# The first gate product of the next slot between the last two down products: one edit of order in a two-block transformer kernel

## The chip, the cores and the metric

The kernel runs on one core of one Trainium2 chip. The metric is the device time of one execution in microseconds (us), as the median of repeated runs. Lower is better.

## The reference, cut to what matters

Sixteen batches of 512 tokens with 128 features pass through two blocks. The change touches only the first:

```
x = x + 0.5 * moe(norm(x))       # shared expert and 16 routed experts, top 2, silu gates
x = x + lin_attn(norm(x))        # linear attention with rotated keys and queries
x = x + 0.5 * moe(norm(x))       # the same weights again
x = x + 0.5 * relu_mlp(norm(x))  # 128 -> 512 -> 128
x = x + softmax_attn(norm(x)); x = x + 0.5 * relu_mlp(norm(x))   # second half of the kernel
```

In the mixture (moe), for one pair of experts or the shared one: `y += (silu(x @ Wg) * (x @ Wu) * routing) @ Wd`. The routing weights come from a sigmoid of the router's logits, the best two of 16, and their share of the sum.

## The kernel before, in words

The front part (`build_front`) does the first four lines above for all batches, the back part the rest. The front is a chain of **slots**. One slot is one mixture layer of one batch (the main work), with the linear attention or the ReLU layer of another batch woven in (the side work). Four slots make a turn: `SIDE = [ATT, MLP, ATT, MLP]`; eight turns make 32 slots, with one slot without side work ahead (number -1) and one behind. Below, "attention slot" and "MLP slot" are named by their side work.

A slot has `NT` = 9 steps, n = 0 to 8: step 0 is the shared expert, steps 1 to 8 a pair of routed experts each. A step has these parts, and each engine's order is written out by hand:

- TensorE (PE): the gate product into bank `G[n % 2]`, the up product into bank `U` (three matmuls of 512 columns each, because the operands are split into a high and a low part), the routing weights of the pair into `C`, and, one step late, the down product of step n-1 (`moe_down`, four transposed matmuls that the trace shows as eight) into `Y`.
- ScalarE (ACT): `s = silu(G)`, line 514.
- VectorE (DVE): `su = U * s` (`activated`, line 668, which writes `h[0]` in step 0), then `h = C * su` (`routed`, line 677).

Around them stand, for the side work of the same slot: row statistics of `xw` on DVE (`side_parts`, line 565, and `total`, line 572), the power on GpSimd (POOL, lines 384 to 390), `zs` on ACT (line 473), `side_transposes` on PE (line 875), `xhs` on ACT, `xls` on DVE (line 690), and then the products that read `xhs` and `xls` (`kvu_product`, line 899, in an attention slot; `hidden`, line 832, into `S[1]` in an MLP slot, followed by `mlp_down` into `S[0]` two steps later). For the main work of the next slot: statistics (`main_stats`), `z` on POOL (lines 377 to 399), `main_transposes` on PE (line 817) in step 3 of an attention slot and step 4 of an MLP slot, `xh`, `xl`, the router logits, their `exp` on ACT (`scores`, line 469), and the top-two choice on DVE (`routing_scores` to `routing_weights`, lines 605 to 654), which ends in `comb_transposes` on PE (line 857) in step 0 of the next slot. `main_residual` (line 681) closes the slot on DVE; `side_parts` of the next slot follows it there.

Every engine takes its instructions strictly in the written order, and semaphores carry the waits between engines: `gate_ready`, `act_done`, `up_ready`, `up_used`, `h_ready`, `down_done` count steps.

Of the kernel before, what the change touches and what calls it, by code (L numbers as in the profile page):

```python
# [33 lines left out]
NT = TE + 1  # L34
FT = 4
# [116 lines left out]
def build_front(nc, weights, early, x_dram, mid_dram, ident_dram, staged_dram, tail_dram, turns):  # L152
    w = weights
    with ExitStack() as ctx:
# [301 lines left out]
        @block.scalar  # L456
        def _(act):
            def main_high(q, i):

                act.wait_ge(zT_ready.sem, zT_ready.at(i, q + 1))  # L460
                nc.scalar.activation(xh[q % 2][:], Z[:], ACT.Copy).then_inc(xh_ready.sem, 1)

            def logits_half(q, i):
                act.wait_ge(logits_ready.sem, logits_ready.at(i, q + 1))
                nc.scalar.activation(lb[:], Z[:, :, E:2 * E], ACT.Copy).then_inc(lb_ready.sem, 1)

            def scores(q, i):
                act.wait_ge(lg_ready.sem, lg_ready.at(i, q + 1))
                nc.scalar.activation(en[:], lg[:], ACT.Exp, scale=-1.0).then_inc(score_ready.sem, 1)

            def normalise(out, src, scale, off):
                for t in range(T):
                    ins = nc.scalar.activation(out[:, t], src[:, t], ACT.Identity, bias=off[:, t:t + 1],
                                               scale=scale[:, t:t + 1])
                return ins

            def side_normalise(m, i, k):
                act.wait_ge(srstd_ready.sem, srstd_ready.at(i, k + 1))
                normalise(zs, xw[SIDE_BATCH[m]], rstd_s, off_s).then_inc(sz_ready.sem, 1)

            def out_normalise(a, i):
                act.wait_ge(rstd2_ready.sem, rstd2_ready.at(i, a + 1))
                normalise(on, S[1], rstd2, off2).then_inc(on_ready.sem, 1)

            def side_high(i, k):
                act.wait_ge(szT_ready.sem, szT_ready.at(i, k + 1))
                nc.scalar.activation(xhs[:], S[0][:], ACT.Copy).then_inc(xhs_ready.sem, 1)

            def hidden(m, k, i):
                act.wait_ge(hid_mm.sem, hid_mm.at(i, FT * nth(m) + k + 1))  # L490
                nc.scalar.activation(hs[k % 2][:], S[1][:], ACT.Relu,  # L491
                                     bias=w["b1"][:, k:k + 1]).then_inc(hid_ready.sem, 1)

            def first_batch(n):
                if n == 4:
                    act.wait_ge(first_xt.sem, 1)
                    nc.scalar.activation(xhs[:], Z[:], ACT.Copy).then_inc(first_xh.sem, 1)
                if n == 6:
                    act.wait_ge(first_kp.sem, 1)
                    nc.scalar.activation(early.khi[:], S[0][:], ACT.Copy).then_inc(early.khi_ready.sem, 1)  # L500
                    act.wait_ge(first_qp.sem, 1)
                    nc.scalar.activation(early.qhi[:], S[1][:], ACT.Copy).then_inc(early.qhi_ready.sem, 1)
                if n == 8:
                    act.wait_ge(first_v.sem, 1)
                    nc.scalar.activation(early.va[:, :, :, 0:DH], Z[:].rearrange("p t (h e) -> p t h e", h=H),
                                         ACT.Copy)

            def slot(m, i, side, prepare):
                g0, steps = NT * m, PREPARE[side or MLP]
                for n in range(NT):  # L510
                    act.wait_ge(gate_ready.sem, gate_ready.at(i, g0 + n + 1))
                    if n >= 2:
                        act.wait_ge(up_used.sem, up_used.at(i, g0 + n - 1))
                    nc.scalar.activation(sbuf_s[n % 2][:], G[n % 2][:], ACT.Silu).then_inc(act_done.sem, 1)  # L514
                    if n == 0:
                        act.wait_ge(combT_ready.sem, combT_ready.at(i, m + 1))
                        nc.scalar.activation(cT[m % 2][:], Z[:], ACT.Copy).then_inc(cT_ready.sem, 1)
                    if n == 0 and side == MLP:
                        act.wait_ge(oT_mm.sem, oT_mm.at(i, nth(m - 1) + 1))
                        nc.scalar.activation(oT[:], S[0][:], ACT.Copy).then_inc(oT_ready.sem, 1)  # L520
                    if n == 1 and side:
                        side_normalise(m, i, m)
                    if n == 2 and side:
                        side_high(i, m)
                    if side == ATT:
                        a = nth(m)
                        if n == 4:
                            act.wait_ge(kvu_out.sem, kvu_out.at(i, T * (a + 1)))
                            nc.scalar.activation(kvu[:, :, 0:D], kvu[:, :, 0:D], ACT.Silu).then_inc(ka_ready.sem, 1)
                            act.wait_ge(q_mm.sem, q_mm.at(i, a + 1))  # L530
                            nc.scalar.activation(qa[:], S[1][:], ACT.Silu, bias=w["bq"][:]).then_inc(qa_ready.sem, 1)
                        if n == 7:
                            out_normalise(a, i)
                    elif side == MLP:
                        if 3 <= n < 3 + FT:
                            hidden(m, n - 3, i)
                    if prepare:
                        if n == steps["transpose"]:
                            main_high(m + 1, i)
                        if n == steps["logits"]:  # L540
                            logits_half(m + 1, i)
                        if n == steps["logits"] + 1:
                            scores(m + 1, i)
                    else:
                        first_batch(n)

            main_high(-1, 0)
            logits_half(-1, 0)
            scores(-1, 0)
            slot(-1, 0, None, True)  # L550
            for i in range(turns):
                for m in range(NM):
                    slot(m, i, SIDE[m], True)
            slot(0, turns, None, False)

        @block.vector
        def _(dve):
# [188 lines left out]

            def slot(m, i, side, before, prepare):
                a, steps = nth(m), PREPARE[side or MLP]
                if side:
                    side_parts(m, i)  # L750
                if not prepare:
                    first_stats()
                for n in range(NT):
# [2 lines left out]
                    activated(m, n, i)  # L756
                    if n == 0:
                        if side:
                            total(stats_s, mv_s, smv_ready)
                        if before == MLP:  # L760
                            side_residual(NM - 1 if m == 0 else m - 1, i - 1 if m == 0 else i)
                    else:
                        routed(m, n, i)
# [46 lines left out]
        def _(pe):  # L810
# [121 lines left out]
            def first_batch(n):  # L932
# [9 lines left out]
                if n == 7:  # L942
# [4 lines left out]
                                       skip_group_check=True)  # L947
                    mm.then_inc(first_v.sem, 1)

            def slot(m, i, side, prepare):  # L950
                g0, a, steps = NT * m, nth(m), PREPARE[side or MLP]
                high, low = xh[m % 2], xl[m % 2]
                pe.wait_ge(xl_ready.sem, xl_ready.at(i, m + 1))
                for n in range(NT):
                    if n >= 2:
                        pe.wait_ge(act_done.sem, act_done.at(i, g0 + n - 1))
                    product(G[n % 2], w["wgh"][:, n], w["wgl"][:, n], high, low).then_inc(gate_ready.sem, 1)
                    if n >= 1:
                        pe.wait_ge(up_used.sem, up_used.at(i, g0 + n))
                    product(U, w["wuh"][:, n], w["wul"][:, n], high, low).then_inc(up_ready.sem, 1)  # L960
                    if n == 0:
# [5 lines left out]
                    if n == 1 and side == MLP:  # L967
                        pe.wait_ge(oT_ready.sem, oT_ready.at(i, nth(m - 1) + 1))
                        down(S[1], oT, w["wout"][:], True).then_inc(side_mm.sem, 1)
                    if n == 2 and side:  # L970
                        side_transposes(i, m)
                    if n == 3 and side:
                        side_input(i, m)
# [5 lines left out]
                        if n == 6:  # L979
                            attend(a, i)  # L980
                    if side == MLP:
                        if 5 <= n < 5 + FT:
                            mlp_down(m, n - 5, i)
                        if 3 <= n < 3 + FT:
                            hidden(m, n - 3, i)
# [6 lines left out]
                    if n >= 1:  # L992
                        moe_down(m, n - 1, i)
                    if side == ATT:
                        if n == 4:
                            queries(a, i)
                        if n == 5:
                            keys_values(a, i)
                moe_down(m, NT - 1, i)

            main_transposes(-1, 0)
            logits(-1, 0)
            slot(-1, 0, None, True)
            for i in range(turns):
                for m in range(NM):
# [884 lines left out]
```

## Time and profile before

| | |
|---|---|
| median of 3 runs | 1994.09 us (1993.52 to 1995.16) |
| the profiled execution's own time | 1994.67 us |
| its span in the trace | 1992.6 us, 34534 instructions |
| granted TensorE clock, mean | 0.989 |
| PE busy over the span | 1886.7 us (95%) |
| DVE busy | 1540.8 us (77%) |
| ACT busy | 1176.8 us (59%) |
| POOL busy | 670.6 us (34%) |
| one MLP and one attention slot together, start to start | 66.3 us, the mean of the 15 periods between line 681's first and last start (106.2 to 1100.5 us) |
| window 566 to 632 us, one MLP and one attention slot | PE 64.11, DVE 46.71, ACT 28.83, POOL 23.45 us busy of 66.00; granted clock 1.00 |

The span begins with the first instruction and ends with the last; what lies between span and time is start and end of the execution. The slots of the front lie between about 41 and 1161 us. PE has two rows: the matmuls, whose ends are modelled, and the weight loads (PEld) ahead of them. A wait shows in square brackets with the engine that ended it. Two matmuls that follow each other are best compared by their starts.

### The profile page before, as it was taken

How to read it: one execution, taken by the hardware profiler on the slowest of the kernel's cores; microseconds unless marked ns; L12 is line 12 of the kernel's file. 1: busy time of each engine (PE TensorE's matmuls, PEld its weight loads, DVE VectorE, ACT ScalarE, POOL GpSimd, SP SyncE). 2: the span in 40 equal slices, each digit the busy share in tenths (PEclk: the TensorE clock that was granted, in tenths of full speed). 3: DMA queues.
4: the chain of work that ended last, by engine and by line, in shares of the span. 5: the costliest groups of instructions: out<-in, count | busy, mean ns of one | idle time of the engine just before them, and what ended most of it. 6: DMA issues, size and time to landing. Idle time of an engine off the chain costs nothing. (4 is left out here: it accounts for less than half of the span.)

```text
span 1992.6 us, 34534 instructions
## 1 busy us (share of the span) xinstructions
PE 1886.7 (95%) x12468; PEld 1312.5 (66%) x12468; DVE 1540.8 (77%) x3888; ACT 1176.8 (59%) x2210; POOL 670.6 (34%) x766
## 2 busy tenths in 40 slices
PE   2999999999999999999999989999999999999997
PEld 1888888888888888888888844444444444444443
DVE  5766866686668666866676669999999999999991
ACT  2344444444444444444444428888888888888884
POOL 2333433343334333433343223333333333333311
PEclk9999999999999999999999969999999999999998
DMA  3000000000000000000010022222232222222210
GB/s 131 7 12 1 12 11 12 1 12 12 11 1 11 12 12 1 11 12 12 1 38 6 7 85 86 86 88 90 91 92 86 86 90 93 90 87 86 86 44 11
DMA packets 49992, 85.81 MB, mean 43 GB/s; under 512 B 6752, under 2 KB 11104, under 8 KB 49760
## 3 DMA queue, kind: packets, MB, share of 16 engines
q1 hardware_dynamic: 47920, 81.85, 13.2%
q8 instruction: 99, 1.62, 0.3%
q10 hardware_dynamic: 1904, 1.78, 0.3%
q14 instruction: 69, 0.57, 0.1%
HBM read 49.26 MB, written 34.87 MB: 42 GB/s over the span
## 5 line engine op out<-in xcount | busy, mean ns | idle before, releaser
L1490 DVE TENSOR_REDUCE b_nm<-b_MX 128x1 f32<-128x512 f32 x1024 | 652.0, 684 | 44.6 <-PE b_MX L1598 24.5
L1383 ACT ACTIVATE b_pr<-b_ST 128x512 f32<-128x512 f32 x1024 | 552.4, 611 | 92.0 <-PE b_ST L1586 89.9
L514 ACT ACTIVATE s<-G 128x512 f32<-128x512 f32 x306 | 182.5, 596 | 350.7 <-PE G L834 348.0
L839 PE MATMUL Y<-w_wd,h 128*128 128x128 f32 x2448 | 329.2, 277 | 17.4 <-DVE h L677 16.1
L668 DVE TENSOR_TENSOR su<-U,s 128x512 f32<-128x512 f32 x272 | 187.1, 688 | 191.4 <-PE U L834 112.8
L839 PEld LDWEIGHTS Y<-w_wd,h 128*128 128x128 f32 x2448 | 305.8, 192 | 33.2 <-DVE h L677 23.9
L1598 PE MATMUL b_MX<-b_kt,b_qt 32*128 32x512 f32 x768 | 236.5, 504 | 2.4 <-DVE b_nm L1490 2.4
L1586 PE MATMUL b_ST<-b_qt,b_kt 32*128 32x512 f32 x768 | 214.7, 494 | 2.8 <-ACT b_pr L1383 1.5
L1586 PEld LDWEIGHTS b_ST<-b_qt,b_kt 32*128 32x128 f32 x768 | 83.1, 181 | 195.0 <-ACT b_pr L1383 141.1
L677 DVE TENSOR_TENSOR h<-C,su 128x512 f32<-128x512 f32 x272 | 188.1, 692 | 9.3
L832 PE MATMUL G<-xh,w_wgh 128*128 128x512 f32 x306 | 145.2, 475 | 0.0
L384 POOL TENSOR_TENSOR vpe_s<-mv_s,w_eps 128x4 f32<-128x4 f32 x32 | 6.4, 199 | 404.1 <-DVE mv_s L572 404.1
L1613 PE MATMUL b_PV<-b_pr,e_va 128*32 128x512 f32 x1024 | 138.1, 612 | 0.0
L1613 PE MATMUL b_PV<-b_pr,b_va 128*32 128x512 f32 x1024 | 136.4, 605 | 0.0
L832 PE MATMUL U<-xh,w_wuh 128*128 128x512 f32 x306 | 123.9, 405 | 9.5 <-DVE su L668 9.5
L834 PE MATMUL G<-xl,w_wgh 128*128 128x512 f32 x306 | 121.1, 396 | 0.0
L833 PE MATMUL G<-xh,w_wgl 128*128 128x512 f32 x306 | 121.0, 395 | 0.0
L834 PE MATMUL U<-xl,w_wuh 128*128 128x512 f32 x306 | 120.7, 395 | 0.0
L833 PE MATMUL U<-xh,w_wul 128*128 128x512 f32 x306 | 120.0, 392 | 0.0
L867 PE MATMUL C<-cT,w_pairs 128*128 128x512 f32 x272 | 107.7, 396 | 0.0
L1598 PEld LDWEIGHTS b_MX<-b_kt,b_qt 32*128 32x128 f32 x768 | 95.5, 184 | 10.2 <-DVE b_nm L1490 5.0
L491 ACT ACTIVATE hs<-S,w_b 128x512 f32<-128x512 f32 x64 | 44.0, 687 | 94.6 <-PE S L834 94.6
(295 smaller groups left out, 3705.6 us busy)
## 6 DMA issues: line engine op xcount, KB each, us to landing
b_kt<-staging SPq DMA_DIRECT2D x48, 256.0 KB, 3.1
b_qt<-staging SPq DMA_DIRECT2D x48, 256.0 KB, 3.5
staging<-e_khi SPq DMA_DIRECT2D x32, 256.0 KB, 2.9
staging<-e_qhi SPq DMA_DIRECT2D x32, 256.0 KB, 2.9
xin<-in_x SPq DMA_DIRECT2D x17, 256.0 KB, 2.8
mid<-xo SPq DMA_DIRECT2D x16, 256.0 KB, 2.0
staging<-e_klo SPq DMA_DIRECT2D x16, 256.0 KB, 2.9
staging<-e_qlo SPq DMA_DIRECT2D x16, 256.0 KB, 2.9
```

The lines of the kernel that those rows point to most:

```text
L514: nc.scalar.activation(sbuf_s[n % 2][:], G[n % 2][:], ACT.Silu).then_inc(act_done.sem, 1)
L668: nc.vector.tensor_tensor(out[:], U[:], sbuf_s[n % 2][:], ALU.mult).then_inc(up_used.sem, 1)
L677: nc.vector.tensor_tensor(h[n % 3][:], C[:], su[n % 2][:], ALU.mult).then_inc(h_ready.sem, 1)
L832: pe.matmul(flat(bank), wh, flat(high), start=True, stop=False)
L833: pe.matmul(flat(bank), wl, flat(high), start=False, stop=False)
L834: return pe.matmul(flat(bank), wh, flat(low), start=False, stop=True)
L839: mm = pe.matmul(bank[:, t], hid[:, t], wd, start=(first and t == 0), stop=True, skip_group_check=True)
L1383: nc.scalar.activation(pr[k % 2][:, j], bank[:].rearrange("p a b -> p (a b)"), ACT.Exp, scale=SM_SCALE).then_inc(used["st"].sem, 1)
L1490: nc.vector.tensor_reduce(nm[g % 2][:, c:c + 1], bank[:].rearrange("p a b -> p (a b)"), AX.X, ALU.max).then_inc(used["mx"].sem, 1)
L1586: pe.matmul(flat(bank_of(B, "st", 0, u)), kt_[g][rows_of(j), k % T], flat(qt[g])[rows_of(j)], start=True, stop=True).then_inc(made["st"].s ...
L1598: pe.matmul(flat(bank_of(B, "mx", rel, u)), qt[g][rows_of(j), u // HG % T], flat(kt_[g])[rows_of(j)], start=True, stop=True).then_inc(made ...
L1613: mm = pe.matmul(flat(PV)[rows_of(j)], va[B.parity][:, kt, g * HG + j], pr[k % 2][:, j], start=(kt == 0), stop=(kt == T - 1), skip_group_c ...
```

## The change

Six edits of order, no arithmetic added or removed:

1. PE: the gate product of step 0 of the next slot is issued between the last two down products of this slot (`gate(m + 1, 0, i)` ahead of `moe_down(m, NT - 1, i)`). It waits for `xl` of the next slot and for the silu of step 8, which reads the same bank.
2. ACT: the silu of step 0 waits for `up_used` of the last step before it, because it writes `s[0]`.
3. PE: in an MLP slot the last `mlp_down` moves from behind `C` of step 8 to between the gate and the up product of step 8.
4. PE: in an attention slot `side_transposes` moves from ahead of `moe_down` of step 1 to behind it (both in step 2).
5. ACT: `scores` (the exponential) moves ahead of the side work of its step; in an MLP slot that is ahead of the last `hidden` activation.
6. DVE: `side_parts` moves from ahead of the first product of the slot (`activated`, n = 0) to behind it.

```diff
 (scalar)
+                    elif n == 0 and up_used.at(i, g0) > 0:
+                        act.wait_ge(up_used.sem, up_used.at(i, g0))
                     nc.scalar.activation(sbuf_s[n % 2][:], G[n % 2][:], ACT.Silu).then_inc(act_done.sem, 1)
...
                     if n == 2 and side:
                         side_high(i, m)
+                    if prepare and n == steps["logits"] + 1:
+                        scores(m + 1, i)
...
                         if n == steps["logits"]:
                             logits_half(m + 1, i)
-                        if n == steps["logits"] + 1:
-                            scores(m + 1, i)
 (vector)
-                if side:
-                    side_parts(m, i)
...
                     activated(m, n, i)
                     if n == 0:
                         if side:
+                            side_parts(m, i)
                             total(stats_s, mv_s, smv_ready)
 (tensor)
+            def gate(m, n, i):
+                g0 = NT * m
+                if n >= 2:
+                    pe.wait_ge(act_done.sem, act_done.at(i, g0 + n - 1))
+                elif n == 0:
+                    pe.wait_ge(xl_ready.sem, xl_ready.at(i, m + 1))
+                    if m >= 0:
+                        pe.wait_ge(act_done.sem, act_done.at(i, g0))
+                product(G[n % 2], w["wgh"][:, n], w["wgl"][:, n], xh[m % 2], xl[m % 2]).then_inc(gate_ready.sem, 1)
...
-                pe.wait_ge(xl_ready.sem, xl_ready.at(i, m + 1))
                 for n in range(NT):
-                    if n >= 2:
-                        pe.wait_ge(act_done.sem, act_done.at(i, g0 + n - 1))
-                    product(G[n % 2], w["wgh"][:, n], w["wgl"][:, n], high, low).then_inc(gate_ready.sem, 1)
                     if n >= 1:
+                        gate(m, n, i)
+                        if side == MLP and n == NT - 1:
+                            mlp_down(m, FT - 1, i)
                         pe.wait_ge(up_used.sem, up_used.at(i, g0 + n))
...
-                    if n == 2 and side:
+                    if n == 2 and side == MLP:
                         side_transposes(i, m)
...
-                        if 5 <= n < 5 + FT:
+                        if 5 <= n < 4 + FT:
                             mlp_down(m, n - 5, i)
...
                     if side == ATT:
+                        if n == 2:
+                            side_transposes(i, m)
...
+                if prepare:
+                    gate(m + 1, 0, i)
                 moe_down(m, NT - 1, i)
...
             logits(-1, 0)
+            gate(-1, 0, 0)
             slot(-1, 0, None, True)
```

## Rows read from the trace of the kernel before

**Rows 1.** Waits of PE's weight loads, 0 to 1140 us: total, times, longest.

```profile
PEld Y L839 <- DVE h L677: 23.3, 33, 1.2
PEld U L832 <- DVE su L668: 16.9, 17, 1.0
PEld Z L817 <- POOL z L399: 15.6, 18, 8.9
```

**Rows 2.** Timeline at an attention slot's end: start, duration, engine, line, operation.

```profile
568.15 1.27 POOL L438 TENSOR_TENSOR og<-og,ub 128x512 f32<-128x512 f32 x1
568.57 0.93 DVE L646 TENSOR_TENSOR first<-first,second 128x64 f32<-128x64 f32 x1
568.71 1.16 PE L839 MATMUL Y<-w_wd,h 128*128 128x128 f32 x8 [0.92 <-DVE h L677]
...
570.27 0.68 DVE L681 SCALAR_TENSOR_TENSOR xw<-Y,xw 128x512 f32<-128x512 f32 x1
...
570.99 0.87 DVE L565 BATCH_NORM_STATS2 stats_s<-xw 128x6 f32<-128x128 f32 x4
...
571.78 0.67 DVE L668 TENSOR_TENSOR h<-U,s 128x512 f32<-128x512 f32 x1
...
572.47 0.28 DVE L572 BATCH_NORM_AGGREGATE mv_s<-stats_s 128x2 f32<-128x6 f32 x3
```

**Rows 3.** Timeline of the MLP slot after it, step 4.

```profile
582.82 1.04 POOL L399 TENSOR_TENSOR z<-z,rstd 128x512 f32<-128x512 f32 x1
...
583.91 0.42 PEld L817 LDWEIGHTS Z<-w_ident,z 128*128 128x128 f32 x4 [0.32 <-POOL z L399]
```

**Rows 4.** Timeline of steps 5 to 8 of that MLP slot, and the next slot's start.

```profile
589.77 0.23 DVE L597 TENSOR_TENSOR lg<-Z,lb 128x64 f32<-128x64 f32 x1 [1.40 <-ACT lb L465]
...
593.72 0.69 ACT L491 ACTIVATE hs<-S,w_b 128x512 f32<-128x512 f32 x1 [1.92 <-PE S L834]
...
594.43 1.28 ACT L469 ACT_TABLE_LOAD   x1
...
596.01 0.20 DVE L605 TENSOR_SCALAR en<-en 128x64 f32<-128x64 f32 x1 [2.64 <-ACT en L469]
...
597.74 0.48 PE L832 MATMUL G<-xh,w_wgh 128*128 128x512 f32 x1
...
599.24 0.50 PE L832 MATMUL U<-xh,w_wuh 128*128 128x512 f32 x1 [0.56 <-DVE su L668]
...
602.34 0.97 PEld L839 LDWEIGHTS Y<-w_wd,h 128*128 128x128 f32 x8 [0.27 <-DVE h L677]
...
603.25 0.48 PE L832 MATMUL G<-xh,w_wgh 128*128 128x512 f32 x1
...
604.03 0.40 PE L832 MATMUL U<-xh,w_wuh 128*128 128x512 f32 x1
```

**Rows 5.** Timeline of the attention slot after that, steps 0 to 3.

```profile
606.81 1.05 PE L839 MATMUL Y<-w_wd,h 128*128 128x128 f32 x8
...
607.62 0.48 PE L832 MATMUL G<-xh,w_wgh 128*128 128x512 f32 x1
...
608.18 0.86 DVE L565 BATCH_NORM_STATS2 stats<-xin 128x6 f32<-128x128 f32 x4
...
609.18 0.28 DVE L572 BATCH_NORM_AGGREGATE mv<-stats 128x2 f32<-128x6 f32 x3
...
609.81 0.63 PE L875 MATMUL S<-w_ident,zs 128*128 128x128 f32 x4 [0.33 <-ACT zs L473]
...
611.51 0.68 DVE L690 TENSOR_TENSOR xls<-S,xhs 128x512 fp32r<-128x512 f32 x1
...
612.79 0.33 PE L899 MATMUL S<-w_wkvuh,xhs 128*128 128x384 f32 x1
```

**Rows 6.** ACT's groups in the back part, 1165 to 1992 us: count, busy time, mean ns.

```profile
L1372 ACT ACTIVATE b_hid<-b_MX,w_b 128x512 f32<-128x512 f32 x68 | 48.0, 705 | 5.0 <-PE b_MX L1521 4.8
...
L1383 ACT ACT_TABLE_LOAD x1 | 1.3, 1283 | 0.0
```

## The prediction, made before the change was run

> **What bounds the kernel now.** I read the page first: TensorE is busy 95% of the span, and the diff touches only the front, so the question is what TensorE's few idle moments in the front are. A view of busy shares cannot say it; the waits can, and the list of PE's weight loads says it better than that of the matmuls, since a matmul's modelled end hides a short wait. [rows 1] are that list for the front. The reader is to see three sorts of wait and their counts: the last down product of a slot waits for `h` (33 times, 23.3 us), an up product waits for `su` 17 times (16.9 us), and the transposes of `z` wait for POOL 18 times (15.6 us, of which 8.9 us is one wait at the very start). 17 and 33 say "once per MLP slot" and "once per slot"; 18 less the start and the slot ahead of the turns is again once per MLP slot. So the third wait is the small one, 0.32 us [rows 3], but it says most: it shows that in every MLP slot a chain of other engines arrives at PE just after PE does.
>
> I then read the timeline of one pair (the pairs are alike, so one stands for 16). At an attention slot's end PE starts the last down product at 568.71 after 0.92 us of idling [rows 2]. At an MLP slot's end there are two gaps: the up product of step 8 starts at 599.24, 1.50 us after the gate product's start at 597.74, where a product takes 0.78 from the first start to the next (603.25 to 604.03), so 0.72 is lost; and the last down product is loaded at 602.34 after a wait of 0.27 [rows 4]. In the attention slot, the side transposes wait 0.33 for `zs` at 609.81 [rows 5].
>
> **The chain beside PE.** Behind an attention slot's end, nothing on DVE starts from PE. `main_residual` starts at 570.27, not when `Y` is done (568.71 + 0.8 of starts + 0.4 for the last matmul = 569.9) but when the routing work of `comb` is through; and that was held by POOL: DVE's small product of line 646 took 0.93 us, from 568.57 to 569.50, and POOL's `og` ran to 569.42 [rows 2]. From there it goes on without a pause that PE ends: row statistics, POOL's power, `zs`, the silu of step 2 behind `zs`, `su`, `h`, `xls`, the statistics of the next main batch, POOL again, and `z` is through at 582.82 + 1.04 = 583.86; PE loads it at 583.91 [rows 3]. `og` itself goes back to `attend` in step 6 of the attention slot through statistics, POOL and ACT. So from `attend` to the transposes of `z`, over a third of each pair is a latency chain, and PE's 0.92 us there is slack that this chain makes, wherever PE takes it.
>
> **The change part by part.** Prices first: a gate product 0.78 behind a down product, a down product 0.81 (606.81 to 607.62) [rows 4, 5], `C` 0.23 (a third of a product).
>
> *Attention slot's end, 16 times.* The gate product (0.78) fills the idle 0.92. It waits for the silu of step 8, which has run before `su` and `h` of that step, for which PE waits anyway; so it fits, and the last down product stays at 568.71. The next slot's up product starts about 0.7 earlier. But the chain does not. `main_residual` stays at 570.27. Then `side_parts` no longer stands ahead of `activated`: before, from 570.27 to the end of the aggregates is 572.75 - 570.27 = 2.48 [rows 2]. After, `activated` starts at 570.99 (the up product, started at about 569.6, delivers 0.54 + 0.40 later plus a hop, 570.65, so it is in time), the statistics 0.61 later, and from the start of the four statistics to the end of the aggregates is 609.46 - 608.18 = 1.28 [rows 5]: 0.72 + 0.61 + 1.28 = 2.61. The chain gets 0.13 longer, and arrives at PE at 584.04. PE, 0.7 early, gives it back, 0.3 to 0.4 at the side transposes and the rest at `z`: the price is 0.13 us, **a loss of 0.13 per pair**, not a gain of 0.7. Without edit 6, `activated` would stay at 571.78 and hold the second up product; so edit 6 is what lets PE run ahead, and what lengthens the chain.
>
> *MLP slot, from `z` to the last down product.* The exponential moves into ACT's idle 1.92 ahead of the last `hidden` activation at 593.72: load 1.28 and 0.26 of work make 1.54 [rows 4], and its input is there since 590.00 (589.77 + 0.23). DVE's `routing_scores`, which sat idle 2.64 until 596.01 [rows 4], can run about 2.3 earlier, with POOL idle, so nothing holds it. So `su` of step 7 is no longer late, the up product of step 8 does not wait, and the last but one group of eight small DVE operations no longer stands ahead of `su` of step 8. The work from the gate product at 597.74 to the last down product is then gate 0.78, `mlp_down` 0.81, up 0.78, `C` 0.23, down 0.81, next gate 0.78 = 4.19, against 602.34 - 597.74 = 4.60 now, though it holds a gate product more. `h` of step 8 is ready at 4.03 + a hop: `su` starts at 1.59 + 0.94 + 0.09 = 2.62, and two DVE products of 0.7 follow. No wait, by 0.1. **Gain 0.41 per pair.** Edit 3 alone would cover the up product's gap too, so the two overlap; if the exponential gained nothing, `su` of step 8 would stay where DVE puts it and this term would be 0.
>
> One cost could hide here: whether ACT needs another table for the Relu behind the exponential. In the back part 68 Relus run among the exponentials with one table load in all [rows 6], so no. The Trainium skill (ScalarE: Activation LUTs, "What ACT_TABLE_LOAD costs") puts a switch at 1.28 us of load plus 1.38 us of drain, which would speak against switching in front of `hidden`. Here the load starts at 594.43, 0.02 after the activation before it ended (593.72 + 0.69) [rows 4], so the trace has the first part and not the second. By the page's price, an estimate, the silu of step 7 would come some 2.8 us later than I have it, still about when it runs now, and `su` of step 8 0.1 late: 16 x 0.1 = 1.6 us less of gain.
>
> *MLP slot's end to the attention slot's `kvu` products.* Here the chain starts from PE's last down product. Before, 602.34 to the end of `xls` is 611.51 + 0.68 - 602.34 = 9.85, and PE is there at 612.79, 10.45 [rows 4, 5], with 0.6 of slack. After, PE has one gate product less (0.78, done before) and no wait of 0.33 to 0.5 at the transposes, since edit 4 puts a down product of 0.81 there; it would be there at 9.2. The chain takes 9.85 + 0.13 + 0.05 = 10.03. So PE waits about 0.8 in all, at the transposes and at `xls`, and the **gain is 10.45 - 10.03 = 0.42 per pair**. `z` is asked for a stage later in this slot, with no wait in [rows 1], and stays behind the `kvu` products. From `kvu` to `attend` everything follows PE, and POOL's products, the slowest there, end ahead of PE: unchanged.
>
> *Edges.* The slot ahead of the turns gains the last term once (its exponential had no Relu to wait for). The last MLP slot is followed by a slot that keeps its statistics ahead of `activated`: its second up product waits for that, and the 0.42 turns into about -0.2. The other waits of edits 1 and 2 are met before: 0.
>
> Sum: 16 x (0.41 - 0.13) + 16 x 0.42 - 0.2 = 4.5 + 6.7 - 0.2 = 11.0. I bound the terms: the first between -0.9 (below) and +0.7, the second between 0 and 1.1 (0.72 + 0.27 + a refill of 0.1), the third between -0.3 and 0.8 + 0.42. The profiled time is 1994.67 us, so 1983.6; the median is 0.58 lower and I take the same step: 1994.1 - 11 = **1983.0 us**.
>
> **The rivals.**
>
> *Every filled gap is won* (a reader of the waits alone would say this): 0.7 at the attention end, 1.1 at the MLP end, 0.4 at the side transposes, 2.2 x 16 = 35, giving 1959. Against it stands the wait for `z` [rows 1, 3]: where it is there already, an earlier PE only waits longer. 6%.
>
> *The chain behind an attention slot is not as rigid*: if edit 6 or the port's release starts it earlier by what PE is early, the first term is +0.4 to +0.7 instead of -0.13: 11 + 16 x 0.7 = 22, giving 1972. For it speaks only that the chain has some twenty hops that I add up from one execution. 9%.
>
> *The statistics behind the first product push the whole chain* (the other side). My 0.13 stands on `activated` starting right behind `main_residual`. If it starts as late as now (because the up product or the silu of step 0 is late), the four statistics add their full 0.9: first term -0.9, third -0.3, second +0.41: -0.8 x 16, giving 2007. It decides at 0.5 us of lengthening, where the sum 0.41 - x + 0.55 - x is zero. The up product has 0.3 to spare at the attention end and none at the MLP end. 8%.
>
> *The gain is given back on the way*: the second term is 0 (DVE's order holds `su` of step 8) and half of the third goes to a wait in the attention slot: 16 x (0.2 - 0.13) = 1, giving 1993, no change that can be told. 8%.
>
> **How the numbers follow.** The likeliest, 69%, has its own range of 1979 to 1989 (each of the three terms off by 0.1 to 0.2). A measurement here tells a change from none at about 0.2%, 4 us. Faster: 69 + 6 + 9 = 84%, and a little of it may fall short: 83%. Same 8%, slower 9%. Leaving out the widest two (1959 and 2007) and half a case more, the range is 1971 to 1991.
>
> **What would show it.** After: the gate product of step 0 stands ahead of the last down product; PE's wait for `h` nearly gone at MLP ends, about 0.2 left at attention ends; no wait of an up product for `su` in step 8; the exponential about 2.6 earlier in MLP slots; the wait for `z` grown from 0.32 to 0.5 to 0.9, with a new wait for `zs` in MLP slots and one for `xls` (0.3 to 0.5) ahead of `kvu`; pairs of 65.6 us where they took 66.3. The prediction is wrong if the stretch from `attend` to `z` gets shorter, or if `activated` of step 0 does not follow `main_residual` directly.

## The result and the profile after

The changed kernel takes 1978.8 us (median of 4 runs, 1977.89 to 1979.13) against 1993.8 for the kernel before (1993.52 to 1995.16) beside it: a ratio of 0.9925, 95% interval 0.991 to 0.994, 15.0 us less. Forecast were 11 us less and 1983.0 us.

Three stretches of the profile tell where it went. The first slot's routing is cast (first `combh`) at 42.0 us instead of 44.2, so 2.2 us came from the setup ahead of the slots, which the change does not touch. From there to the last slot's cast it is 1075.5 us instead of 1088.8: 13.3 us, the change's own share. Behind it, 859.4 against 859.6.

The group of `main_residual` (now line 684) gives the period of a pair: durations, first and last start of 16.

```profile
L684 DVE SCALAR_TENSOR_TENSOR xw<-Y,xw x16: 679/683/685, 103.8 to 1085.7; 128x512 f32<-128x512 f32 x16
```

(1085.7 - 103.8) / 15 = 65.46 us, against 66.29: 0.83 less. The 15 periods make 12.4 of the 13.3 us, and the first and the last slots, outside these periods, the other 0.9. The waits of PE's weight loads over the front, 0 to 1130 us (total, times, longest):

```profile
PEld Z L819 <- POOL z L399: 20.9, 18, 9.0
...
PEld S L877 <- issue: 15.1, 32, 0.5
PEld Y L841 <- DVE h L680: 14.1, 33, 0.7
PEld S L901 <- DVE xls L693: 6.6, 16, 0.4
...
PEld Z L859 <- DVE comb L657: 4.5, 16, 0.3
PEld U L834 <- DVE su L671: 4.5, 17, 0.9
```

Beside [rows 1] the reader sees what happened to the filled gaps: the waits for `h` and `su` fell by 9.2 and 12.4 us, and others grew or are new: `z` 5.3 more, `xls` 6.6, `comb` 4.5, and the side transposes (line 877) now wait 32 times, so in every slot; before it was 11.8 us in 16. A wait of a weight load is not the same as idle time of PE, since a weight load runs while the matmul ahead of it does; idle time is read from the starts of the matmuls.

The attention slot's end and the next slot's steps 0 and 4, in the timeline, answering [rows 2, 3]:

```profile
559.87 1.27 POOL L438 TENSOR_TENSOR og<-og,ub 128x512 f32<-128x512 f32 x1
...
560.28 0.94 DVE L649 TENSOR_TENSOR first<-first,second 128x64 f32<-128x64 f32 x1
...
560.42 1.16 PE L841 MATMUL Y<-w_wd,h 128*128 128x128 f32 x8 [0.22 <-DVE h L680]
...
561.99 0.68 DVE L684 SCALAR_TENSOR_TENSOR xw<-Y,xw 128x512 f32<-128x512 f32 x1
562.59 0.68 DVE L671 TENSOR_TENSOR h<-U,s 128x512 f32<-128x512 f32 x1
563.19 0.86 DVE L568 BATCH_NORM_STATS2 stats_s<-xw 128x6 f32<-128x128 f32 x4
...
564.19 0.28 DVE L575 BATCH_NORM_AGGREGATE mv_s<-stats_s 128x2 f32<-128x6 f32 x3
...
575.57 0.31 PEld L819 LDWEIGHTS Z<-w_ident,z 128*128 128x128 f32 x3 [0.66 <-POOL z L399]
```

PE's wait ahead of the last down product shrank from 0.92 to 0.22, as the gate product now fills it; but from `main_residual` to `z`'s weight load it is 13.58 us (561.99 to 575.57), and was 13.64 [rows 2, 3]. The wait for `z` doubled, 0.32 to 0.66. The starts of the matmuls around it give PE's own share of that wait, before and after:

```profile
583.64 0.40 PE L834 MATMUL S<-xls,w_w1h 128*128 128x512 f32 x1
583.92 0.66 PE L817 MATMUL Z<-w_ident,z 128*128 128x128 f32 x4
...
574.96 0.40 PE L836 MATMUL S<-xls,w_w1h 128*128 128x512 f32 x1
575.57 0.66 PE L819 MATMUL Z<-w_ident,z 128*128 128x128 f32 x4 [0.22 <-POOL z L399]
```

In the rows just ahead of these one matmul follows the next in 0.23 to 0.24. Here it is 0.28 before and 0.61 after, so PE lost 0.04 before and 0.37 after: in the kernel before, PE and the chain met almost exactly, and that is why an earlier PE gained next to nothing here. The MLP slot's end and the attention slot behind it, answering [rows 4]:

```profile
583.47 1.28 ACT L469 ACT_TABLE_LOAD   x1
...
585.38 0.69 ACT L491 ACTIVATE hs<-S,w_b 128x512 f32<-128x512 f32 x1 [0.35 <-PE S L836]
586.09 1.28 ACT L517 ACT_TABLE_LOAD   x1
587.38 0.60 ACT L517 ACTIVATE s<-G 128x512 f32<-128x512 f32 x1
...
593.48 0.97 PEld L841 LDWEIGHTS Y<-w_wd,h 128*128 128x128 f32 x8 [0.18 <-DVE h L680]
...
594.68 0.69 DVE L684 SCALAR_TENSOR_TENSOR xw<-Y,xin 128x512 f32<-128x512 f32 x1 [0.27 <-PE Y L841]
...
595.45 0.69 DVE L671 TENSOR_TENSOR h<-U,s 128x512 f32<-128x512 f32 x1
596.05 0.86 DVE L568 BATCH_NORM_STATS2 stats_s<-xw 128x6 f32<-128x128 f32 x4
...
597.05 0.28 DVE L575 BATCH_NORM_AGGREGATE mv_s<-stats_s 128x2 f32<-128x6 f32 x3
```

The exponential's table is loaded 1.9 us ahead of the last `hidden` activation, where it stood 0.7 behind its start, and the Relu needs no table of its own. No drain shows: the second load begins 0.02 us after the Relu's end, and the silu 0.01 us after the load's. The up product of step 8 has no wait left (590.98, 0.81 behind the start of the `mlp_down` that now stands ahead of it).

For everything below, one pair is cut at four places of PE, by the first start of the `attend` products, of the transposes of `z` in the MLP slot, of its last down product, and of the `kvu` products. Periods over 15 pairs agree with these sums to 0.05. The column "first cast" is where the setup ends in that kernel's profile; it differs by up to 2.9 us, so small differences of the medians are better judged by the pairs.

| kernel | attend to z | z to last down | last down to kvu | kvu to attend | pair | first cast | median us |
|---|---|---|---|---|---|---|---|
| before | 24.00 | 18.42 | 10.45 | 13.42 | 66.29 | 44.2 | 1993.8 |
| changed | 23.94 | 18.02 | 9.97 | 13.53 | 65.46 | 42.0 | 1978.8 |
| no_gate | 24.41 | 17.92 | 10.77 | 13.55 | 66.65 | 42.5 | 1998.5 |
| no_exp | 23.92 | 18.43 | 10.08 | 13.53 | 65.96 | 41.7 | 1986.6 |
| no_stats | 23.95 | 18.00 | 9.83 | 13.50 | 65.28 | 42.8 | 1977.5 |
| no_side | 23.95 | 18.01 | 10.52 | 13.42 | 65.90 | 43.1 | 1985.3 |
| no_down | 23.92 | 17.99 | 9.98 | 13.55 | 65.44 | 41.6 | 1979.6 |
| no_exp_down | 23.94 | 18.86 | 9.99 | 13.53 | 66.32 | 44.3 | 1993.9 |
| long_off | 24.56 | 18.00 | 10.28 | 13.53 | 66.37 | 42.8 | 1993.6 |
| neg | 23.89 | 18.02 | 9.66 | 13.54 | 65.11 | 44.5 | 1974.2 |
| neg_side | 23.60 | 17.99 | 9.68 | 13.53 | 64.80 | 43.8 | 1969.9 |
| neg_side_no_stats | 23.95 | 17.99 | 9.85 | 13.51 | 65.30 | 44.0 | 1977.4 |
| neg_share | 23.41 | 18.03 | 9.66 | 13.54 | 64.64 | 44.5 | 1967.2 |

### The profile page after: what moved, and what is told of

It reads as the page before. It is cut to its first block and busy times, and to the rows that moved or that the text cites. A ratio compares the mean times of both kernels' runs of the same rounds, so it can differ in the third digit from the quotient of the medians.

```text
span 1976.9 us, 34600 instructions
## 1 busy us (share of the span) xinstructions
PE 1889.2 (96%) x12468; PEld 1308.3 (66%) x12468; DVE 1542.2 (78%) x3888; ACT 1179.2 (60%) x2210; POOL 670.7 (34%) x766
## 3 DMA queue, kind: packets, MB, share of 16 engines
q1 hardware_dynamic: 47920, 81.85, 13.3%
## 5 line engine op out<-in xcount | busy, mean ns | idle before, releaser
L473 ACT ACTIVATE zs<-xw,off_s,rstd_s 128x128 f32<-128x128 f32 x128 | 52.8, 483 | 66.7 <-POOL off_s L390 66.7
```

## The experiments

### Undoing one edit at a time

The title names edit 1; the change that was measured is all six, so they are undone one by one. Edit 2 only keeps `s[0]` from being overwritten too early and was not undone.

**Edit 1, the early gate product (no_gate).**

```diff
-                if prepare:
-                    gate(m + 1, 0, i)
                 moe_down(m, NT - 1, i)
+                if prepare:
+                    gate(m + 1, 0, i)
```

> The changed kernel with edit 1 alone undone: the first gate product of a slot stands behind the last down product again. Everything else as changed. Theory A (a latency chain beside PE sets each slot's end to start): without it the up product of step 0, and with it the first DVE product and the side statistics behind it, come 0.5 us later after an attention slot and 0.8 us later after an MLP slot, both inside the chain; so 16 x 1.2 = 19 us slower than the changed kernel, about 1998 us, slower than the kernel before. Theory B (the gate product only fills PE's idle time): 0.7 us per attention slot's end is lost, 11 us, about 1990 us.

Measured: 1998.47 us (1995.42 to 2000.2), ratio to before 1.002 (1.0011 to 1.0029). That is 20 us slower than the changed kernel and slower than the kernel before. The pair is 1.19 us longer, which is more than the 0.7 us of idling that the gate product fills. In its timeline, at an attention slot's end and at an MLP slot's end:

```profile
571.68 0.69 DVE L684 SCALAR_TENSOR_TENSOR xw<-Y,xw 128x512 f32<-128x512 f32 x1
572.78 0.69 DVE L671 TENSOR_TENSOR h<-U,s 128x512 f32<-128x512 f32 x1 [0.41 <-ACT s L517]
...
604.87 0.69 DVE L684 SCALAR_TENSOR_TENSOR xw<-Y,xin 128x512 f32<-128x512 f32 x1 [0.27 <-PE Y L841]
606.34 0.69 DVE L671 TENSOR_TENSOR h<-U,s 128x512 f32<-128x512 f32 x1 [0.77 <-PE U L836]
```

From `main_residual` to the first DVE product it is 1.10 and 1.47 us where the changed kernel has 0.60 and 0.77, and the statistics stand behind that product. The table has both delays: 0.47 more from `attend` to `z` for the first (0.50), 0.80 more from the last down product to `kvu` for the second (0.70, and `main_residual` 1.20 behind that product's start instead of 1.09), and 0.10 less between. So the whole loss is the chain, and this is the rival "the statistics behind the first product push the whole chain", made real. That it is edit 6 which makes the loss of edit 1 so dear is argued from these rows; no run leaves both out.

**Edit 5, the early exponential (no_exp).**

```diff
-                    if prepare and n == steps["logits"] + 1:
-                        scores(m + 1, i)
...
                         if n == steps["logits"]:
                             logits_half(m + 1, i)
+                        if n == steps["logits"] + 1:
+                            scores(m + 1, i)
```

> The changed kernel with edit 5 alone undone: the exponential stands behind the last hidden activation of the MLP slot again. Theory A: su of step 8 is held by the late routing operations on DVE, the last down product of an MLP slot comes 0.4 us later; 16 x 0.4 = 6.5 us slower than the changed kernel, about 1985 us. Theory B (the moved mlp_down already fills that gap, edit 5 is without effect): 1979 us.

Measured: 1986.64 us (1984.85 to 1986.91), ratio 0.9961 (0.9948 to 0.9974), 7.8 us slower than the changed kernel. The table has 0.41 of it between `z` and the last down product, 18.43 for 18.02, and 0.11 between that and `kvu`. There the down product starts out of a wait for `h` again, and `main_residual` follows its start in 1.20 us, as in the kernel before, where the changed kernel has 1.09.

**Edit 6, side statistics behind the first product (no_stats).**

```diff
+                if side:
+                    side_parts(m, i)
...
                     if n == 0:
                         if side:
-                            side_parts(m, i)
                             total(stats_s, mv_s, smv_ready)
```

> The changed kernel with edit 6 alone undone: the side statistics stand ahead of the slot's first DVE product again. Theory A: the trace of the changed kernel has 2.48 us from the start of main_residual to the end of the aggregates, as before, so the chain is as long either way; the second up product waits about 0.5 to 0.9 us, but PE would wait for the chain later anyway. 0 to 3 us slower than the changed kernel, 1979 to 1982 us. Theory C (as the prediction has it, the edit lengthens the chain by 0.13): 0 to 4 us faster, 1975 to 1979. Theory B: PE's wait is lost in full, 32 x 0.5 = 16 us, 1995 us.

Measured: 1977.51 us (1977.2 to 1978.14), ratio 0.9917 (0.9902 to 0.9932). The two intervals overlap, so the times alone do not tell it from the changed kernel; the pair is 0.17 us shorter (65.29 by the period), while its setup ended 0.8 later. Its timeline at the MLP slot's end:

```profile
594.85 0.69 DVE L684 SCALAR_TENSOR_TENSOR xw<-Y,xin 128x512 f32<-128x512 f32 x1 [0.27 <-PE Y L842]
595.57 0.87 DVE L568 BATCH_NORM_STATS2 stats_s<-xw 128x6 f32<-128x128 f32 x4
...
597.05 0.28 DVE L575 BATCH_NORM_AGGREGATE mv_s<-stats_s 128x2 f32<-128x6 f32 x3
```

2.48 us from `main_residual` to the end of the aggregates (597.33), against 2.65 in the changed kernel, where the first product starts 0.77 instead of 0.60 behind `main_residual`, since it had to wait for its up product; and the `kvu` products come 9.83 instead of 9.97 behind the last down product. At the attention slot's end both have 2.48. So the edit lengthens the chain by 0.17 in one place and by nothing in the other. The second up product does wait for DVE here (0.30 and 0.44 us), and it costs nothing, since PE would wait further on.

**Edit 4, side transposes behind the down product (no_side).**

```diff
-                    if n == 2 and side == MLP:
+                    if n == 2 and side:
                         side_transposes(i, m)
...
-                        if n == 2:
-                            side_transposes(i, m)
```

> The changed kernel with edit 4 alone undone: in attention slots the side transposes stand ahead of the down product of step 1 again. Theory A: the transposes cannot start before zs is ready, so the down product (0.8 us), now behind them, pushes the kvu products; of it 0.37 us are covered by the present wait for xls, the rest, 0.5 us per attention slot, is lost: 8 us, about 1987 us. Rival: the chain through xls sets kvu anyway, no loss, 1979 us.

Measured: 1985.33 us (1984.21 to 1986.36), ratio 0.9955 (0.9938 to 0.9972), 6.5 us slower. The stretch to `kvu` is 10.52 for 9.97, `kvu` now comes 0.60 behind the end of `xls` instead of 0.05, and 0.11 of it comes back behind it (13.42 for 13.53).

**Edit 3, and edits 3 and 5 together (no_down, no_exp_down).**

```diff
-                        if side == MLP and n == NT - 1:
-                            mlp_down(m, FT - 1, i)
...
-                        if 5 <= n < 4 + FT:
+                        if 5 <= n < 5 + FT:
```

> The changed kernel with edit 3 alone undone: the last mlp_down stands behind C of step 8 again. Theory A: with the exponential early there is no gap left for it to fill, and DVE's two products of step 8 are early enough; no difference, 1977 to 1980 us. Theory B (it fills PE's idle time of 0.7 us): 16 x 0.7 = 11 us slower, 1990 us.

Measured: 1979.6 us (1977.82 to 1981.82), ratio 0.993 (0.9915 to 0.9945): no difference.

> The changed kernel with edits 3 and 5 undone. Theory A: either edit alone covers the gap ahead of the up product of step 8, together undone it is back (0.7 us), and the gate product of the next slot no longer fits in the short wait ahead of the last down product. Undoing 5 alone cost 7.8 us; this one should cost 7 us more, about 1993 us. If the two do not overlap: the sum of the single ones, that of edit 5 (7.8 us) plus that of edit 3 measured beside this.

Measured: 1993.87 us (1990.77 to 1996.65), ratio 1.0 (0.999 to 1.0009). Undone together the two cost 15.1 us, alone 7.8 and 0.8. They cover the same gap: each alone suffices to keep the up product of step 8 from waiting, and only edit 5 frees DVE. With neither, the wait is back as it was in [rows 4]:

```profile
599.83 0.50 PE L834 MATMUL U<-xh,w_wuh 128*128 128x512 f32 x1 [0.56 <-DVE su L671]
```

and the early gate product then stands in front of a last down product that had only 0.27 us to wait, which makes `z` to last down 18.86, longer than in the kernel before. The table's 0.86 per pair make 13.8 us of it; in this kernel's profile the setup also ends 2.3 us later than in the changed kernel's.

### The chain itself, longer and shorter

**One more small POOL operation (long_off).**

```diff
                 own.step(nc.gpsimd.tensor_tensor(off[:], mean_var[:, :, 0], scale[:], ALU.mult))
                 own.settle()
+                own.step(nc.gpsimd.tensor_scalar(off[:], off[:], 1.0, None, ALU.mult))
+                own.settle()
                 nc.gpsimd.tensor_scalar(off[:], off[:], -1.0, None, ALU.mult).then_inc(done.sem, 1)
```

> The changed kernel with one more small POOL operation (a multiplication by 1.0 of 128x4 values, 0.28 us with its wait) in each of the two places that make scale and offset: once per slot for the side statistics, once per attention slot behind attend. Nothing else is added, and PE, DVE and ACT do the same work. Theory A (the latency chain sets the time of each pair): 2 x 0.28 between attend and the transposes of z, and 0.28 between the last down product of an MLP slot and the kvu products: 0.84 us per pair, 13 us slower, about 1992 us. Theory B (PE's work sets it, waits are only filled): POOL is 34% busy, no change, 1979 us.

Measured: 1993.63 us (1992.08 to 1995.2), ratio 0.9998 (0.9989 to 1.0008). 48 operations of 0.2 us on an engine that is 34% busy cost 14.8 us, as much as the whole change had brought: 0.91 per pair by the period, where 3 x 0.28 = 0.84 were expected; the table has 0.62 between `attend` and `z` and 0.31 ahead of `kvu`. This settles that in the changed kernel latency sets these two stretches, and that PE's work does not.

**The negated mean made by ACT while POOL takes the power (neg, neg_side, neg_share).**

```diff
 (scalar, side_normalise; out_normalise likewise)
+                act.wait_ge(smv_ready.sem, smv_ready.at(i, k + 1))
+                nc.scalar.activation(nmean_s[:], mv_s[:, :, 0], ACT.Copy, scale=-1.0).then_inc(sneg.sem, 1)
                 act.wait_ge(srstd_ready.sem, srstd_ready.at(i, k + 1))
 (gpsimd)
-                own.step(nc.gpsimd.tensor_tensor(off[:], mean_var[:, :, 0], scale[:], ALU.mult))
-                own.settle()
-                nc.gpsimd.tensor_scalar(off[:], off[:], -1.0, None, ALU.mult).then_inc(done.sem, 1)
+                pool.wait_ge(sneg.sem, negated)
+                nc.gpsimd.tensor_tensor(off[:], nmean_s[:], scale[:], ALU.mult).then_inc(done.sem, 1)
```

The GpSimd lines are those of neg_side; neg and neg_share hand the semaphore and the tile (`nmean_s` or `nmean2`) to the same function as arguments.

> The changed kernel with the chain made shorter: the negated mean is made by ACT while POOL takes the power, so POOL's last multiplication by -1 (0.28 us with its wait) leaves the chain at both places. All six edits stay. Theory A: the same 0.84 us per pair the other way, as far as PE's waits reach (0.7 to 1.0 us between attend and z, 0.6 us in the attention slot): 13 us faster, about 1965.5 us, which beats both kernels. Theory B: no change, 1979 us, or slower by ACT's 48 small operations if these stand in the way.

Measured: 1974.15 us (1970.97 to 1975.83), ratio 0.99 (0.9886 to 0.9915). It beats both kernels, but gives 4.7 us instead of 13, and the table says where it fails: ahead of `kvu` the 0.31 came, between `attend` and `z` only 0.05 instead of 0.56. (In its profile the setup also ended 2.5 us later than in the changed kernel's.) Its timeline at the attention slot's end:

```profile
558.64 1.28 POOL L441 TENSOR_TENSOR og<-on,uw 128x512 f32<-128x512 f32 x1 [1.62 <-ACT on L478]
...
558.66 1.34 DVE L654 TENSOR_TENSOR share<-sc,den 128x64 f32<-128x64 f32 x1
559.93 0.68 DVE L680 TENSOR_TENSOR su<-U,s 128x512 f32<-128x512 f32 x1
```

`share`, 0.22 us elsewhere, took 1.34: it came 0.02 us behind the start of POOL's `og` and ended 0.08 behind `og`'s end, and `su` of step 8 stood behind it. So it is in every attention slot of this profile. The last down product came 9.30 behind `attend`, and 8.79 in the changed kernel. In the changed kernel `og` starts 6.88 behind `attend` and `share` has just passed. It is the same meeting as that of line 646 in [rows 2], which also ended 0.08 behind `og`'s end. The Trainium skill (SBUF — State Buffer, "Who interferes with whom") says that a DVE instruction with two SBUF inputs contends with a GpSimd instruction that reads SBUF, and that the port pair they share is an exclusive lock; this case's traces agree: 1.34 us here, 0.93 in the kernel before and 0.94 in the changed one (lines 646 and 649), for operations of 0.22.

neg_side keeps the shorter way only for the side statistics, so that `og` stays where it was:

> As the kernel with ACT's negated mean, but only for the side statistics; the scale and offset behind attend are made as before. In that kernel POOL's first product of og came 0.3 us earlier and fell on the last small DVE operation of the routing (share), which then took 1.34 us instead of 0.22 and held su of step 8. Theory A with the shared port: without that collision both shortened places count in full, 0.28 us each per pair, 16 x 0.56 = 9 us faster than the changed kernel, about 1970 us, faster than with both places shortened. Theory A without the port: half of what the both-places kernel gave, 1976 to 1977 us.

Measured: 1969.86 us (1969.53 to 1970.43), ratio 0.9881 (0.9866 to 0.9896), 8.9 us faster than the changed kernel: one shortened place less, and 4.3 us faster than with both.

neg_share keeps both and moves the operation out of the way:

```diff
 (vector, routing_next)
-                own.settle(1)
-                step(nc.vector.tensor_tensor(share[:], sc[:], wide(den), ALU.mult))
 (vector, routing_weights)
-                own.settle(1)
+                own.settle()
+                step(nc.vector.tensor_tensor(share[:], sc[:], wide(den), ALU.mult))
                 step(nc.vector.tensor_tensor(first[:], first[:], second[:], ALU.add))
```

> ACT's negated mean at both places, and the share operation moved from the end of routing_next to the start of routing_weights, behind h of step 8, so that POOL's og can't hold su of step 8. Theory of the shared port: the last down product of an attention slot starts about 8.5 us after attend (9.30 with the collision, 8.79 in the changed kernel), share's own 0.26 us come back in the routing chain; the pair takes about 64.9 us, 1969 us. If the port is not the cause, the down product stays at 9.3 and the time at 1974 us.

Measured: 1967.16 us (1964.49 to 1967.9), ratio 0.9865 (0.985 to 0.9879), the fastest version here: 26.6 us below the kernel before. The last down product starts 8.47 behind `attend`. The pair is 64.64, 0.3 better than expected; in its timeline the moved operation waits for `og` (0.95 us) in place of the one behind it, `og` ends 0.31 earlier behind `attend` than in the changed kernel (9.20 for 9.51), and `main_residual` starts 0.17 earlier (10.19 for 10.36), so that the move costs 0.14 of the 0.31.

**Edit 6 beside the shorter chain (neg_side_no_stats)**, neg_side with `side_parts` put back as above:

> The kernel before this one with edit 6 undone (side statistics ahead of the first DVE product). Theory D: edit 6 costs 0.17 us of chain per pair, but lets PE run further ahead; with the shorter chain the second up product's wait (0.3 to 0.44 us) is no longer hidden, and the gain is limited to PE's remaining waits, 0.1 at z and 0.2 at kvu: about 1972 us, no faster than with edit 6. Rival: edit 6 is a plain cost of 0.17 x 16, and undoing it gives 1967 us here as well.

Measured: 1977.35 us (1976.89 to 1978.44), ratio 0.992 (0.9903 to 0.9936), 7.5 us slower than neg_side and no faster than no_stats. More than expected: the shorter chain gives nothing at all. Its PE rows show where the waits went, and so do the waits of the weight loads:

```profile
564.17 0.51 PE L850 MATMUL U<-xh,w_wuh 128*128 128x512 f32 x1 [0.30 <-DVE h L686]
596.87 0.51 PE L850 MATMUL U<-xh,w_wuh 128*128 128x512 f32 x1 [0.44 <-DVE h L686]
```

```profile
PEld U L850 <- DVE h L686: 27.1, 33, 1.2
...
PEld Z L835 <- POOL z L411: 15.4, 18, 8.9
```

With the statistics in front, PE is held at the second up product by a chain that the POOL operation is not part of. From that up product to the last matmul ahead of the transposes of `z` it is 11.08 us in this kernel and in no_stats alike (means over the pairs), though the chain beside it is shorter in one of them, so this is PE's own work; and it takes as long as the old chain did: `attend` to `z` is 23.95 in both. So edit 6, a small cost in the changed kernel, is worth 0.48 us per pair once the rest of the chain is shorter.

### The setup

before_twin is the kernel before, unchanged.

> The kernel before, unchanged in every instruction, profiled once more for the setup ahead of the first slot. In the profiles so far the first slot's routing is cast at 41.6 to 44.5 us, and in the kernel before at 44.2, in the changed kernel at 42.0. If that is a matter of the single execution (DVE and POOL meet in the setup), this one lies anywhere in 41.5 to 44.5 us, with the pair at 66.29 us all the same. If it belongs to the program, it is 44.2 again.

Measured: one run of 1994.59 us; first cast at 44.2 us again, pair 66.29. The profiles of the other kernels have it at 41.6 to 44.5, with the slots' code different but the setup's the same. That equal programs gave an equal start speaks for something fixed with the program, but the inside of the two setups differs (the DVE operation of line 1773, on 512 columns, took 2.73 us in the one and 0.43 in the other), and one pair of profiles is little. What sets these 2.2 us stays open.

## Why the prediction was right, and where its sizes were off

The direction, the mechanism and the range held; the time was 4.2 us below the forecast, about half of it from a setup that no step spoke of and half from the size of the terms. Point by point:

**The chain beside PE** was right, and carried the forecast. Filled gaps did come back as waits for `z`, `xls` and `zs`. long_off shows it directly, and the rival "every filled gap is won" is out: the attention slot's end, with 0.7 us less idling on PE, gave 0.06 per pair. The wait of 0.32 for `z` in [rows 3] was read as PE ahead of the chain; by the matmul starts PE was ahead by 0.04. The conclusion stands, since an earlier PE could only wait.

**The attention slot's end: -0.13 forecast, +0.06 measured.** The mis-sized term was the lengthening of the chain by edit 6. I had `activated` 0.72 behind `main_residual`, the spacing of the statistics in [rows 2]; a product follows in 0.60, so that from `main_residual` to the end of the aggregates it stays 2.48. That accounts for 0.13 of the 0.19. The other 0.06 lie where the prediction had "a pause that PE ends" ruled out: `su` of step 2 starts 6.75 behind `main_residual` before and 6.67 after.

```profile
576.53 0.40 PE L834 MATMUL U<-xl,w_wuh 128*128 128x512 f32 x1
577.02 0.69 DVE L668 TENSOR_TENSOR su<-U,s 128x512 f32<-128x512 f32 x1 [1.39 <-ACT s L514]
...
568.66 0.69 DVE L671 TENSOR_TENSOR su<-U,s 128x512 f32<-128x512 f32 x1 [1.95 <-ACT s L517]
```

The silu that `su` reads ends 6.64 behind `main_residual` in both; in the kernel before, the end of PE's up product, as the profile models it, is 576.93, 0.02 after the silu's, and in the changed kernel it is 0.6 ahead of the silu's. By these rows PE held this place by a little, and an earlier PE won that little; no run separates it. The prediction's own sign of being wrong, a shorter stretch from `attend` to `z`, thus came up, by 0.06 of 24 us; the chain that yields by 0.4 to 0.7, for which the sign was set up, did not.

**The MLP slot, `z` to the last down product: 0.41 forecast, 0.40 measured.** That edits 3 and 5 overlap held too (0.8, 7.8 and 15.1 us). The bound "0 if the exponential gained nothing" held: no_exp has 18.43 there, and the kernel before 18.42.

**To `kvu`: 0.42 forecast; 0.48 measured, of which 0.11 is lost again before `attend`**, net 0.37. The chain was 0.17 longer at this end, against 0.13 forecast, but began 0.1 earlier behind a down product that no longer stalls (`main_residual` 1.09 behind its start instead of 1.20). The 0.11 I had put at 0; it is absent in no_side too, where `kvu` does not wait for `xls`, so it comes together with PE's wait ahead of `kvu`, but no run shows why.

**The sum**: 0.83 per pair instead of 0.70, 13.3 us instead of 11.0, and 2.2 us of setup which no step spoke of.

**The part played by edit 6.** "Edit 6 is what lets PE run ahead" is false as a gain for the changed kernel: to leave it out costs nothing, because PE only runs ahead into a wait. It is true for neg_side.

**The 8% rival** (statistics behind a late first product, 2007 us) did not occur, but its mechanism is real: no_gate is it, with 0.5 and 0.7 us of delay, at 1998 us.

**The price of a table switch in the Trainium skill** (ScalarE: Activation LUTs, "What ACT_TABLE_LOAD costs": 1.28 us of load and 1.38 us of drain) shows in its first part and not in its second in the changed kernel either: the silu of step 7 starts 0.01 us behind its table load (587.37 to 587.38).

## What to carry to other kernels

Where an in-order engine is 95% busy and every filled gap is followed by another wait, cut the loop at the waits and ask which chain of other engines arrives there; its length, not the busy engine's work, may set the period, and an operation of 0.2 us in it counts once per pass. Edits of order are worth what their neighbours leave them: two covered the same gap, the change without its first edit was slower than the kernel before, and one paid only when the chain had become shorter, so a sum over edits measured alone would have misled. When a chain gets shorter, look at what its operations will now meet on the other engines. And read PE's idle time from the starts of its matmuls: a weight load can wait 0.3 us where PE loses 0.04.

## What was not expected of the hardware

- A DVE operation of 0.22 us with both inputs in SBUF took 1.34 us when it came 0.02 us behind the start of a POOL product, and 0.22 when it came just ahead. A shift of 0.3 us brought this about once per pair: the kernel with it (neg) is 7.0 us slower than the one with the operation moved out of the way (neg_share).
- A second DVE operation on 512 columns starts 0.60 us behind the start of the first, though each is shown as 0.68 to 0.69 us; statistics of what the first wrote start 0.72 us behind it.
- The setup of the same code ended at 41.6 to 44.5 us in the profiles of thirteen programs.
